# Layer norms issued with less lead: instruction order in a two-layer attention and feed-forward kernel

## What is computed

```
x = x + attn0a(norm(x));  x = ffn0(x)      # with adapters (LoRA)
x = x + attn0b(norm(x));  x = ffn0(x)
x = x + attn1a(norm(x));  x = ffn1(x)      # 8 experts, top 2
x = x + attn1b(norm(x));  x = ffn1(x)
norm(x) = (x - mean) / sqrt(var + eps)     # before each block
```

## Time and profile before

| what | value |
|---|---|
| time, median of 3 runs | 2205.06 us (2204.71 to 2205.49) |
| the profiled execution's own time | 2205.49 us |
| its span in the profile | 2203.7 us |
| mean granted PE clock | 0.965 of full |
| end of the first norm (last L127 starts) | 23.80 us |
| ffn1_after_a, from its last base addition to its last L127 | 1834.75 to 1864.42 us |
| ffn1_after_b, last base addition starts | 2190.22 us |

### The profile page before, as it was taken

One profiled execution on the slowest core, in us unless ns is written; L12 is line 12 of the kernel. 1 busy time (PEld: TensorE's weight loads), 2 busy tenths in 40 slices (PEclk: granted clock), 3 DMA queues, 4 the chain that ended last, 5 costly groups with the idle time before them and its releaser, 6 DMA issues. The chain is left out here.

```text
span 2203.7 us, 33255 instructions
## 1 busy us (share of the span) xinstructions
PE 2051.8 (93%) x11536; PEld 1469.4 (67%) x11536; DVE 1391.7 (63%) x2509; ACT 1164.9 (53%) x2691; POOL 831.8 (38%) x1011
## 2 busy tenths in 40 slices
PE   6999988989999999999988789999999987999988
PEld 4333356777888888888866667777777665744457
DVE  6888474546666666666655646666666557667756
ACT  5777553255656656656544555555555534345553
POOL 0000100144635545555340145545554421847611
PEclk8999989999999999999998899999999999989999
DMA  3000022751112111121011344344333221833301
GB/s 120 1 1 1 4 96 89 223 185 39 48 39 68 35 53 52 35 68 39 30 39 51 91 112 110 92 106 115 92 92 73 61 69 31 224 77 73 72 25 39
DMA packets 95732, 158.10 MB, mean 72 GB/s; under 512 B 12063, under 2 KB 33567, under 8 KB 93390
## 3 DMA queue, kind: packets, MB, share of 16 engines
q1 hardware_dynamic: 85774, 134.19, 21.6%
q0 software_dynamic: 9792, 21.77, 4.0%
HBM read 90.91 MB, written 31.46 MB: 56 GB/s over the span
## 5 line engine op out<-in xcount | busy, mean ns | idle before, releaser
L2566 POOL TENSOR_TENSOR attn1a_probs<-attn1a_probs,attn1a_recip 128x128 f32<-128x128 f32 (+3 forms) x256 | 179.2, 721 | 233.0 <-DVE attn1a_recip L2749 232.4
L1916 POOL TENSOR_TENSOR attn0b_probs<-attn0b_probs,attn0b_recip 128x128 f32<-128x128 f32 (+3 forms) x256 | 196.5, 789 | 185.1 <-DVE attn0b_recip L2160 185.0
L2620 ACT ACTIVATE attn1a_probs<-attn1a_scores,attn1a_negmax 128x128 f32<-128x128 f32 (+3 forms) x256 | 132.9, 524 | 173.7 <-DVE attn1a_negmax L2735 172.5
L2020 ACT ACTIVATE attn0b_probs<-attn0b_scores,attn0b_negmax 128x128 f32<-128x128 f32 (+3 forms) x256 | 133.0, 525 | 122.5 <-DVE attn0b_negmax L2153 122.0
L1467 DVE TENSOR_REDUCE attn0a_negmax<-attn0a_by_query 128x2 f32<-128x1024 f32 x128 | 151.9, 1219 | 10.1 <-PE attn0a_by_query L1584 10.1
L2735 DVE TENSOR_REDUCE attn1a_negmax<-attn1a_scores 128x2 f32<-128x256 f32 (+3 forms) x128 | 105.4, 824 | 68.9 <-PE attn1a_scores L2940 68.9
L1909 POOL TENSOR_TENSOR attn0b_q_cos<-attn0b_q_cos,attn0b_q_swap 128x512 f32<-128x512 f32 x64 | 84.3, 1317 | 159.5 <-DVE attn0b_q_swap L2142 159.5
L2028 ACT ACTIVATE attn0b_probsT_hi<-attn0b_turned 128x256 fp32r<-128x256 f32 (+3 forms) x128 | 90.2, 705 | 88.2 <-PE attn0b_turned L2304 86.6
L2153 DVE TENSOR_REDUCE attn0b_negmax<-attn0b_scores 128x2 f32<-128x256 f32 (+3 forms) x128 | 105.0, 821 | 46.8 <-PE attn0b_scores L2293 46.8
L2952 PE MATMUL attn1a_turned<-ident_f,attn1a_probs 128*128 128x128 f32 x640 | 116.1, 279 | 8.8 <-DVE attn1a_probsT L2743 7.5
L2139 DVE TENSOR_TENSOR attn0b_q_cos<-attn0b_aux,attn0b_cos_q 128x512 f32<-128x512 f32 x60 | 41.5, 692 | 116.0 <-ACT attn0b_q_swap L2041 116.0
(11 more groups left out here) (539 smaller groups left out, 6191.9 us busy)
## 6 DMA issues: line engine op xcount, KB each, us to landing
pre<-in_b_o SPq DMA_DIRECT2D x16, 1024.0 KB, 5.6
attn1a_qT<-attn1a_stage SPq DMA_DIRECT2D x128, 128.0 KB, 3.1
attn1a_qT<-attn1a_stage SPq DMA_DIRECT2D x64, 256.0 KB, 3.9
attn0b_vals<-attn0b_v_out SPq DMA_DIRECT2D x16, 512.0 KB, 4.0
attn0b_keys<-attn0b_part SPq DMA_DIRECT2D x32, 256.0 KB, 4.2
pre<-in_b_q SPq DMA_DIRECT2D x8, 1024.0 KB, 7.6
attn0b_kT<-attn0b_keys SPq DMA_DIRECT2D x64, 128.0 KB, 2.8
pre<-in_b_kv SPq DMA_DIRECT2D x5, 1024.0 KB, 6.3
```

The costliest lines, as they stand in the source:

```text
L1916: pool.tensor_tensor(x, x, recip[:, r % DEEP, e:e + 1].broadcast_to([P, (qt + 1) * P]), ALU.mult).then_inc(s_scaled, 1)
L2020: act.activation(probs[:, r % DEEP, e, 0:width], scores[r % 2][:, e, 0:width], ACT.Exp, bias=negmax[:, r % 2, e:e + 1], accum_out=sums[:, ...
L2566: pool.tensor_tensor(x, x, recip[:, r % DEEP, e:e + 1].broadcast_to([P, (qt + 1) * P]), ALU.mult).then_inc(s_scaled, 1)
L2620: act.activation(probs[:, r % DEEP, e, 0:width], scores[r % 2][:, e, 0:width], ACT.Exp, bias=negmax[:, r % 2, e:e + 1], accum_out=sums[:, ...
```

## The change

The diff moves calls in two functions; no instruction is added or taken out, and no size changes.

- In attn0a, ACT took root(t + 1) ahead of normalise(t); now it takes root(t), normalise(t), hi(t - 1). DVE took statistics two tiles and factors one tile ahead of the tile that ACT normalises; now each is one tile nearer.
- In ffn1_after_a, ACT took the roots of the second norm up to three tiles ahead of hi(t); now root and normalise of a tile stand together (`scaled`), and the first two tiles stand ahead of weighted_hi(1). PE transposes tiles 0 and 1 of the second norm ahead of experts(4), where it did tile 0 ahead of experts(4) and tile 1 ahead of experts(5).
- In both ffn1 blocks DVE takes add(1) ahead of share(1), and weighted_lo(1) ahead of add(2). In ffn1_after_a, factors(1) stands ahead of weighted_lo(1), and the order of adds, factors and second_lo behind is written out by hand.

```diff
--- before.py
+++ after.py
@@ -607,21 +607,15 @@
                     odds(0)
             weighted_hi(0)
             odds(1)
-            if project:
-                weighted_hi(1)
-            else:
-                second.root(act, m, 0)
-                second.root(act, m, 1)
-                second.normalise(act, m, 0)
-                weighted_hi(1)
-                second.root(act, m, 2)
-                second.normalise(act, m, 1)
+            if not project:
+                scaled(second, 0)
+                scaled(second, 1)
+            weighted_hi(1)
+            if not project:
                 for t in range(TILES):
-                    if t + 3 < TILES:
-                        second.root(act, m, t + 3)
                     second.hi(act, t, final(m.xnT_hi, t))
                     if t + 2 < TILES:
-                        second.normalise(act, m, t + 2)
+                        scaled(second, t + 2)
 
         @block.vector
         def _(dve):
@@ -789,19 +783,31 @@
             choose_second(1)
             add_base(7)
             add(0)
+            add(1)
             share(1)
-            add(1)
             factors(0)
+            factors(1)
+            weighted_lo(1)
             add(2)
-            weighted_lo(1)
-            factors(1)
             add(3)
-            for t in range(TILES):
-                second_lo(t)
-                if t + 2 < TILES:
-                    factors(t + 2)
-                if t + 4 < TILES:
-                    add(t + 4)
+            second_lo(0)
+            factors(2)
+            second_lo(1)
+            factors(3)
+            add(4)
+            second_lo(2)
+            add(5)
+            factors(4)
+            second_lo(3)
+            add(6)
+            factors(5)
+            second_lo(4)
+            factors(6)
+            second_lo(5)
+            add(7)
+            factors(7)
+            second_lo(6)
+            second_lo(7)
 
         @block.tensor
         def _(pe):
@@ -910,10 +916,13 @@
             for t in range(HALF):
                 experts(t)
             turn_weighted(1)
+            if not project:
+                second.turn(pe, m, 0)
+                second.turn(pe, m, 1)
             for t in range(HALF, TILES):
-                if not project:
-                    second.turn(pe, m, t - HALF)
                 experts(t)
+                if not project and 5 <= t < 7:
+                    second.turn(pe, m, t - 3)
             if not project:
                 for t in range(4, TILES):
                     second.turn(pe, m, t)
@@ -1319,11 +1328,9 @@
         @block.scalar
         def _(act):
             act.wait_ge(s_eps, 1)
-            norm.root(act, m, 0)
             for t in range(TILES + 1):
-                if t + 1 < TILES:
-                    norm.root(act, m, t + 1)
                 if t < TILES:
+                    norm.root(act, m, t)
                     norm.normalise(act, m, t)
                 if t >= 1:
                     norm.hi(act, t - 1, m.xnT_hi[:, :, bass.ts(t - 1, P)])
@@ -1422,13 +1429,11 @@
                 norm.statistics(dve, m, t)
 
             statistics(0)
-            statistics(1)
-            norm.factors(dve, 0)
             for t in range(TILES + 1):
-                if t + 2 < TILES:
-                    statistics(t + 2)
                 if t + 1 < TILES:
-                    norm.factors(dve, t + 1)
+                    statistics(t + 1)
+                if t < TILES:
+                    norm.factors(dve, t)
                 if t >= 1:
                     norm.lo(dve, t - 1, m.xnT_lo[:, :, bass.ts(t - 1, P)], m.xnT_hi[:, :, bass.ts(t - 1, P)])
                 if t == 4:
```

## The result

The changed kernel takes 2219.71 us (median of 6 runs, 2213.21 to 2223.74), the kernel before 2204.76 us beside it (6 runs, 2203.50 to 2205.49). The ratio is 1.0068, interval 1.0053 to 1.0083: slower by 15.0 us (11.7 to 18.3). The forecast was 2216.4, range 2212.5 to 2220, so the median lies 0.3 us inside its upper end. The profiled execution took 2219.8 (span 2218.1), 14.3 more than that of before.

The account below looks back on a forecast made before the run. Bound in the changed stretches: chains of small steps between ACT and DVE, with PE waiting. 7.5 (first norm) + 0.7 (clock) + 2.6 (ffn1_after_a tail) + 0.5 (ffn1_after_b) = 11.3 us on 2205.06: 2216.4, range 2212.5 to 2220.

Parts of the forecast that it names:

- First norm, +7.5: First norm in attn0a: the turn closes at 3.11 us a tile against 1.66, so PE's turn(7) comes 7.5 us later.
- the 0.7 of clock: Behind the first norm's turn(7): three more of the 42 matmuls run at PE's lower clock level, 0.7 us.
- Tail, +2.6: Tail of ffn1_after_a: DVE waits for hi in four turns, and the last lo comes 2.6 us later.
- the walk: Tail of ffn1_after_a: each step's start worked out in the new order, ending with the last lo at 1866.97 against 1864.42.
- the four turns of the prediction: Tail of ffn1_after_a: four turns in which DVE was expected to wait for hi.
- Last block, +0.5: Tail of ffn1_after_b: share(1) stands behind one more add, so the experts and last adds come 0.5 us later.
- Its doubt about the stores: End of ffn1_after_b: the stores bunch a little more, which could add as much again as the 0.5 us.
- The shorter tail: Rival in ffn1_after_a: the tail gets shorter, half of DVE's 7.1 us of waits go; +5.2, 2210.3 us; chance 0.07.
- the open first norm: Rival: the first norm doesn't close its turn; not slower, together -3.0, 2202.1 us; chance 0.03, divided between no change and faster.
- PE at its lower level through all 42 matmuls: Rival behind the first norm: 10.1 us of clock in place of 0.7, +20.7, 2225.8 us; chance 0.04.
- the first rival: Rival in ffn1_after_a: the tail gets shorter as the chain root, hi, lo, add breaks; +5.2, 2210.3 us; chance 0.07.
- a difference arising inside the attention blocks: Sign that the prediction is wrong: time differing inside the attention blocks, of which the change touches nothing; no size given.

Follow-up runs that it names:

- e9_after_busy: The changed kernel plus 8 matmuls on PE ahead of turn(7) in ffn1_after_a's tail: 2220.05 us against 2207.91 for the kernel before, ratio 1.0053.
- e10_after_again: The changed kernel itself, measured once more: 2221.22 us against 2207.91 for the kernel before, ratio 1.0056.
- e1_norm: The kernel before with only the first norm in attn0a changed, both ACT and DVE order: 2215.75 us against 2206.11, ratio 1.0042.
- e6_norm_dve: The kernel before with only DVE's order in the first norm changed, ACT's root still a tile early: 2214.23 us, ratio 1.0040.
- e4_root: The kernel before with only ACT's root in ffn1_after_a moved behind hi(t), DVE and PE order kept: 2202.06 us against 2206.11, ratio 0.9982.
- e2_tail: The kernel before with only ffn1_after_a changed, all of ACT's, DVE's and PE's order there: 2212.67 us against 2206.11, ratio 1.0032.
- e8_tail_again: The kernel before with only ffn1_after_a changed, measured once more without added matmuls: 2211.40 us, ratio 1.0021 to the kernel before.
- e7_tail_busy: The kernel before with only ffn1_after_a changed, plus 8 matmuls on PE ahead of turn(7): 2207.90 us, ratio 1.0006 to the kernel before.
- e11_first_busy: The changed kernel plus 6 and 4 matmuls on PE behind turn(4) and turn(5) of the first norm: 2222.61 us against 2205.95 before, ratio 1.0075.
- e3_last: The kernel before with only ffn1_after_b's DVE order changed: 2205.54 us against 2206.11, ratio 0.9998.

## Why the prediction was right, point by point

**First norm, +7.5 and the 0.7 of clock: right.** The steps from start to start gave a turn of 3.11 us; it is 3.12. From normalise(0) (6.91, the loads being 0.31 earlier in that execution) to the last 21.68 us, worked out 21.51. turn(7) is 29.46 + 0.31 - 22.08 = 7.7 later, forecast 7.5. Four matmuls at the lower level instead of one cost 8.17 - 7.38 = 0.8, forecast 0.7. That the clock's term came out so near is luck: with the same norm it was 0.8 to 1.4 us (four matmuls in e9_after_busy, five in e10_after_again, seven in e1_norm), and with DVE's order alone 0.1 (one, in e6_norm_dve). e6_norm_dve shows which engine's order does the rest.

**Tail, +2.6: right, step by step.** With the 9.30 us of the start added, the walk's starts meet the trace: weighted_hi(1) 1852.17 (1852.20), add(3) 1854.93 (1854.96), lo(3) 1865.00 (1865.01), last lo 1876.27 (1876.34). The 2.5 us that the prediction had DVE idle ahead of add(2) are 2.43. lo(1), lo(3), lo(4) and lo(5) wait 1.36 us each for hi, the four turns of the prediction, and lo(6) behind add(7) a fifth time.

**Last block, +0.5: right** (0.53; alone 0.51). Its doubt about the stores is not settled: their end moves by as much without the change.

**Rivals.** The shorter tail and the open first norm are ruled out by the same rows, PE at its lower level through all 42 matmuls by the row at 32.08. But the first rival named a real possibility: the tail is 4.8 us shorter if only the root moves. e4_root and e2_tail have the same loop on ACT and differ on DVE (and in PE's turns and ACT's first steps). hi(t) stands behind normalise(t + 1) and so behind factors(t + 1). In e4_root an add with its statistics, 1.55 us, stands between these factors and lo(t). In the changed order lo(1), lo(3), lo(4), lo(5) and lo(6) have them straight ahead, and these five are the ones that wait 1.36 us; lo(2), which has add(4) between, doesn't wait. Which of the differences weighs how much was not tried.

**What was mis-sized is the clock.** The sum had it in one place, for 0.7 us. The whole change measured +15.0 (11.7 to 18.3), and again +12.4 (9.3 to 15.5) and +11.7 to +16.5 in its two variants, against 11.3. That the median of the first measurement lies inside the range is partly luck: it is 0.3 us from the end, and three of its six runs are above 2220. Two more places have been seen. The idle time ahead of turn(7) of ffn1_after_a cost the kernel with that tail alone 2.9 +- 1.8 us over all runs (e8_tail_again against e7_tail_busy), of which the traces show about 1 us; I had worked out this idle time, since the walk puts turn(7) 2.6 us later with no more work for PE, and had not asked what PE does in it. And the later rise at 69 us cost 1.5 us in all four profiles of kernels with the whole change, and in neither of the two with the first norm alone (64 to 66 us). Since e1_norm and the changed kernel run the same instructions up to there, I can't say whether this is the change's or a chance of four executions: that stays open. So does the rest of the +15.0; the second measurement's interval goes down to 9.3, which leaves no rest, and the step of 3.0 us at the end of attn1b, which e10_after_again and e11_first_busy have and the changed kernel's profile has not, comes and goes without the change. The prediction also said that a difference arising inside the attention blocks would make it wrong; these 1.5 us are such a one.

The Trainium skill (TensorE: Matmul & The Clock Gate, A second HAM failure mode: psum-queue depth-cycling) says of another kernel that a PE which pauses often between groups of matmuls swings between its two levels. This trace agrees for the tail, where PE went to 0.63 us matmuls and back between turn(4) and turn(6) in one execution and behind turn(7) in another.

## What to carry to other kernels

When two in-order engines pass small steps back and forth, write the turn down as a string of starts: if an instruction that releases the next tile (here the next statistics and factors, behind a lo) stands behind one that waits for this tile, the turn is closed, and its length is the sum of all steps on both engines instead of the larger share. Move the waiting small instruction alone and leave the other engine's lead in place: the same root, moved by itself, gained 4 us; moved together with DVE's order it made the tail 2.6 us longer and the kernel 4.4 to 9.7 us slower (2.6 to 6.6 when measured again). And where an edit makes a busy TensorE wait some 2 us more, price also the matmuls behind that wait at the lower level; useful work placed there, or even useless work, can be cheaper than idleness, if it lasts until the wait ends and no longer. And before a microsecond in a pair of traces is given to an edit, look for the same step in the trace of a kernel without that edit: the largest one behind the tail here was also in e3_last.

## What the runs showed of the hardware

- TensorE fell from 2.4 to 1.2 GHz over single idle times of 2.24 us in this tail (four of four profiles), and did not over 1.11 us or less there (nine of nine). The length of one idle time does not settle it, though: in before's tail the clock stayed up over 1.99 us ahead of turn(3) and fell within the 2.01 us ahead of turn(4). In the first norm it fell behind pauses of 1.94 and 0.95 us with four transposes and three matmuls between them.
- With PE as busy and the same instructions ahead, the clock fell at the end of attn1b in some executions and not in others (granted 1.00 and 0.62 from 2110 to 2115 us in before and e3_last), for 2.3 to 3.0 us.
- One kernel's executions differ by whole clock episodes: the kernel before took 2203.3 to 2210.0 us in 23 runs on one chip, and 2203.5 to 2205.5 in its first six. A median of six can thus be off by a microsecond or two, as much as the terms at issue here.
- The hand-overs between engines, start to start, repeated within 0.03 us almost throughout: offset to a waiting normalise 0.19 to 0.20, hi to a waiting lo 0.60 to 0.63, root to a waiting reciprocal 0.31 to 0.33. Each trace has one exception to the first (1.05) and one to the second (0.70). A walk of 26 us made from them was 0.07 off at its end.
